# A vision tower with a mixture of experts: gate turns and bias products become stages of TensorE's order

## What is computed

```python
x2 = layernorm(x, ln2_g, ln2_b).reshape(B * S, H)
probs = softmax(x2 @ wr)                      # 64 experts
gate_v, gate_i = top_k(probs, 2)              # two experts for each token
pos = ...                                     # the token's place in its expert's buffer
buf = zeros((E, C, H)).at[ef, posc].add(tok)  # C = 72 rows for each expert
h = gelu(einsum('ech,ehf->ecf', buf, w1) + b1[:, None, :])
y = einsum('ecf,efh->ech', h, w2) + b2[:, None, :]
moe_out = (y[ef, posc] * (gf * keep)[:, None]).reshape(T, TOP_K, H).sum(axis=1)
```

## Time and profile before

| | |
|---|---|
| median of 3 runs | 390.56 us (388.23 to 392.81) |
| profiled execution | 389.98 us, of which the span of the core 388.3 |
| granted TensorE clock, mean | 0.959 |
| busy: PE, DVE, ACT, POOL | 347.7, 233.7, 220.9, 197.4 us |
| DMA | 50.20 MB, mean 129 GB/s |

### The profile page before, as it was taken

How to read it: one execution, slowest core, us unless ns; L and a number is a source line. 1 busy time by engine, 2 the same in 40 slices (tenths; PEclk the granted TensorE clock), 3 DMA queues, 4 the chain that set the end, 5 groups by cost and what they waited for, 6 DMA issues and landing times.

```text
span 388.3 us, 11371 instructions
## 1 busy us (share of the span) xinstructions
PE 347.7 (90%) x4424; PEld 315.2 (81%) x4424; DVE 233.7 (60%) x615; ACT 220.9 (57%) x640; POOL 197.4 (51%) x312
## 2 busy tenths in 40 slices
PE   8969799999988999997899899499999999999950
PEld 8748687887866889696778788399999999999950
DVE  1446788763489899897868985623335433333314
ACT  1247677777659876677488563103555555555520
POOL 3169687587841112236345767720555555555550
PEclk9999999999999999998999999559999999999995
DMA  7999924000000000000000100037899989999206
GB/s 277 374 391 334 150 28 125 2 2 1 2 3 0 3 3 2 3 2 3 3 3 2 33 9 13 15 95 202 272 320 316 322 308 316 327 324 314 85 9 182
DMA packets 21239, 50.20 MB, mean 129 GB/s; under 512 B 4116, under 2 KB 10340, under 8 KB 21058
## 3 DMA queue, kind: packets, MB, share of 16 engines
q1 hardware_dynamic: 18146, 46.96, 37.9%
q0 software_dynamic: 3040, 2.52, 2.4%
HBM read 43.97 MB, written 7.72 MB: 133 GB/s over the span
## 4 chain that ended last, share of the span: by engine, by line
PE 57%; DVE 12%; ACT 11%; POOL 9%; DMA 6%; issue 4%; SPq 1%; POOLq 0%; DVEq 0%
PE bank L728 34%; PE scores L728 18%; DMA lambdas<-in_lambdas 4%; ACT work L1037 4%; PE bank L803 3%; ACT norm L1037 3%; POOL rstd L613 3%; DVE mx L1266 2%; DVE stats L1203 2%; DVE work L1275 1%; ACT src L1037 1%; PE bank L979 1%; POOL rstd L611 1%; ACT xrow L1037 1%; POOL norm L664 1%
## 5 line engine op out<-in xcount | busy, mean ns | idle before, releaser
L1037 ACT ACTIVATE work<-scores,b1T 128x72 f32<-128x72 f32 x256 | 61.3, 322 | 66.9 <-PE scores L728 66.9
L728 PE MATMUL bank<-ring,work 128*72 128x128 f32 x512 | 97.3, 274 | 0.0
L720 POOL DMA_INDIRECT expert_rows<-work,put_u x64 | 59.9, 935 | 61.7 <-issue 37.7
L728 PE MATMUL scores<-work,ring 128*128 128x72 f32 x512 | 89.0, 258 | 0.2 <-ACT work L1037 0.2
L728 PEld LDWEIGHTS scores<-work,ring 128*128 128x128 f32 x512 | 76.9, 191 | 0.3 <-issue 0.3
L728 PE MATMUL bank<-wT 128*128 128x128 f32 x504 | 72.3, 283 | 2.7 <-ACT work L1037 2.7
L728 PEld LDWEIGHTS bank<-wT 128*128 128x128 f32 x504 | 63.8, 193 | 5.7 <-ACT work L1037 3.1
L1037 ACT ACTIVATE work<-bank 128x288 f32<-128x288 f32 (+3 forms) x136 | 46.7, 376 | 34.4 <-PE bank L728 27.0
L1437 DVE TENSOR_SCALAR work<-bank,work 72x128 f32<-72x128 f32 x64 | 22.2, 347 | 67.5 <-PE bank L728 67.5
L728 PEld LDWEIGHTS bank<-ring,work 128*72 128x72 f32 x512 | 53.8, 145 | 0.2 <-ACT work L1037 0.2
L611 POOL TENSOR_SCALAR rstd<-mv 96x3 f32<-96x3 f32 x32 | 10.1, 315 | 54.8 <-DVE mv L1206 53.6
(11 more groups left out here) (159 smaller groups left out, 594.2 us busy)
## 6 DMA issues: line engine op xcount, KB each, us to landing
ring<-in_experts SPq DMA_DIRECT2D x64, 512.0 KB, 5.0
work<-in_patches SPq DMA_DIRECT2D x3, 864.0 KB, 10.6
slot_rows<-hid SPq DMA_DIRECT2D x1, 2340.0 KB, 30.2
work<-slot_rows SPq DMA_DIRECT2D x7, 292.5 KB
wT<-in_weights SPq DMA_DIRECT2D x1, 1664.0 KB, 13.9
expert_rows<-mid POOLq DMA_DIRECT2D x2, 576.0 KB, 5.1
ring<-expert_rows SPq DMA_DIRECT2D x4, 288.0 KB, 4.0
expert_rows<-work,put_u POOLq DMA_INDIRECT x64, 4.4
```

Of the source, the lines that this page charges most:

```text
L720: pool.indirect_dma_start(out=ytok[:, :], out_offset=bass.IndirectOffsetOnAxis(ap=put_u[:, e:e + 1], axis=0), in_=ys[0:CAP, e % NY, :], in ...
L728: return nc.tensor.matmul(o, a, b, start=start, stop=stop)
L1037: return nc.scalar.activation(o, i, f, **kw)
```

## The change

The gate turns and bias products become two stages, gate_turn and gate_bias, in TensorE's order. Those of batches 0, 1 and 2 stand before rt_count:3, except the product of batch 2, right behind it; those of batch 3 follow. Turns use two banks of `scores` by turns, products 0 and 1 two others, and products 2 and 3 the banks 0 and 1 once their last jobs are taken. ScalarE instead of DVE copies the turned gates. Two tables of unread matmuls change: six instead of ten ahead of rt_turn:3 and two new ones ahead of rt_count:3; and behind each of the six row writes four instead of three, at the end ten instead of four. The waits of the expert loop on the bias sums follow the new banks.

```diff
-HEAD_WARM = 4
-PACE = 3
+HEAD_WARM = 10
+PACE = 4
...
-    moe_v:3 rt_turn:2 rt_logits:2 moe_flip:3 moe_pv:3 moe_out:3 rt_count:2 rt_turn:3 rt_logits:3 rt_count:3
+    moe_v:3 rt_turn:2 rt_logits:2 moe_flip:3 moe_pv:3 moe_out:3 rt_count:2 gate_turn:0 gate_turn:1 rt_turn:3 rt_logits:3 gate_turn:2 gate_bias:0 gate_bias:1 rt_count:3 gate_bias:2 gate_turn:3 gate_bias:3
...
-    moe_out:3=2 rt_count:2=9 rt_turn:3=10 rt_logits:3=3
+    moe_out:3=2 rt_count:2=9 rt_turn:3=6 rt_logits:3=3 rt_count:3=2
...
+            def spare(i):
+
+                name, count = taken(jobs[[n for n in range(len(jobs)) if n % 4 == i][-1]])
+                pe.wait_ge(S[name], count)
+                return banks[i]
...
+                elif stage == "gate_turn":
+
+                    pe.wait_ge(S["exp_in"], len(soft_n))
+                    pe.wait_ge(S["gm_ready"], b + 1)
+                    if b >= 2:
+                        pe.wait_ge(S["gmT_ready"], b - 1)
+                    for i in range(TPB):
+                        last = nc.tensor.transpose(scores[0:E, b % 2, TP * i:TP * i + TP], gm[:, TPB * b + i, :], const("ident")[0:TP, 0:TP])
+                    last.then_inc(S["gm_turned"], 1)
+                elif stage == "gate_bias":
+
+                    pe.wait_ge(S["gmT_ready"], b + 1)
+                    o = scores[:, 2 + b, :] if b < 2 else spare(b - 2)
+                    for i in range(TPB):
+                        last = mm(o[0:TP, D * i:D * i + D], gmT[:, b, TP * i:TP * i + TP], b2nat[:, :])
+                    last.then_inc(S["bias_full"], 1)
...
-            bias_turn(0)
-            bias_turn(1)
-            bias(0, banks[0])
-            bias_turn(2)
-            bias(1, banks[1])
-            bias_turn(3)
-            bias(2, scores[:, 2, :])
-            bias(3, scores[:, 3, :])
+            pe.wait_ge(S["gmT_ready"], NB)
...
-                        pe.wait_ge(S["bias_added"], 3)
+                        pe.wait_ge(S["bias_added"], 1)
...
-                    pe.wait_ge(S["bias_added"], min(f + 1, 2))
+                    pe.wait_ge(S["bias_added"], min(f + 3, 4))
...
+                elif stage == "gate_turn":
+                    act.wait_ge(S["gm_turned"], b + 1)
+                    go(gmT[:, b, :], scores[0:E, b % 2, 0:TB]).then_inc(S["gmT_ready"], 1)
...
-            for b in range(NB):
-                bias_in(b)
             dve.wait_ge(last_sent[2 * TPB - 1], 16)
-            bias_add(0, banks[0])
-            bias_add(1, banks[1])
-            bias_add(2, scores[:, 2, :])
-            bias_add(3, scores[:, 3, :])
+            bias_add(0, scores[:, 2, :])
+            bias_add(1, scores[:, 3, :])
+            bias_add(2, banks[0])
+            bias_add(3, banks[1])
```

More of the change, by code:

```diff
@@ L206 @@
     moe_v:2 rt_gate:0 moe_norm_b:3 rt_norm_b:1 moe_turn:3 rt_turn:1 rt_logits:1 moe_qk:3 rt_gate:1 moe_flip:2
-    moe_pv:2 moe_scores:3 rt_norm_b:2 moe_v:3 rt_turn:2 rt_logits:2 moe_flip:3 rt_gate:2 moe_pv:3 rt_norm_b:3
-    rt_turn:3 rt_logits:3 rt_gate:3
+    moe_pv:2 moe_scores:3 rt_norm_b:2 moe_v:3 rt_turn:2 rt_logits:2 moe_flip:3 rt_gate:2 moe_pv:3 gate_turn:0 gate_turn:1 rt_norm_b:3
+    rt_turn:3 rt_logits:3 gate_turn:2 rt_gate:3 gate_turn:3
     """,
@@ L956, in _ @@
                     last.then_inc(filled(job), 1)
-            def bias_turn(b):
-                pe.wait_ge(S["gm_ready"], b + 1)
-                if b >= 1:
-                    pe.wait_ge(S["gmT_ready"], b)
-                for i in range(TPB):
-                    last = nc.tensor.transpose(scores[0:E, 3, TP * i:TP * i + TP], gm[:, TPB * b + i, :], const("ident")[0:TP, 0:TP])
-                last.then_inc(S["gm_turned"], 1)
-            def bias(b, o):
-                pe.wait_ge(S["gmT_ready"], b + 1)
-                for i in range(TPB):
-                    last = mm(o[0:TP, D * i:D * i + D], gmT[:, b, TP * i:TP * i + TP], b2nat[:, :])
-                last.then_inc(S["bias_full"], 1)
             def x_turn(e):
@@ L1388, in _ @@
                     v.tensor_tensor(gm[:, t, :], oh[:, t, 0, :], oh[:, t, 1, :], ALU.add).then_inc(S["gm_ready"], 1)
-            def bias_in(b):
-                dve.wait_ge(S["gm_turned"], b + 1)
-                v.tensor_copy(gmT[:, b, :], scores[0:E, 3, 0:TB]).then_inc(S["gmT_ready"], 1)
             def bias_add(b, o):
```

## The result

The changed kernel takes 386.48 us (median of 20 runs, 383.62 to 391.43), the kernel before 390.65 us in the same session (20 runs, 388.23 to 393.46). The ratio is 0.991, with a 95% interval of 0.989 to 0.993: a gain of 3.7 us, between 2.9 and 4.5. The ratio leaves out executions in a slower state, which three of the changed kernel's showed; the quotient of the two medians, which leaves out none, is 0.989. That is within 1% or at its edge; within 1% was forecast. It is a little more than the 2.8 us of the sum. The profiled execution of after took 384.09 us against 389.98.

The account below looks back on a forecast made before the run. The start of the expert stage, set by TensorE's unread matmuls behind the last row write, was taken as the bound. Starting them at 251.0 gains 2.9 us, less 0.1 for a later count: 387.5 us predicted, range 385.6 to 390.2.

Parts of the forecast that it names:

- the sum: Start of the experts: unread matmuls from 251.0 end at 261.1 instead of 263.95; gain 2.9 less 0.1, so 2.8 us.
- items 3, 4 and 5: The first of these: turn 2 and products 0 and 1 fit TensorE's 2.88 us idle before the last count, hidden by 0.4.
- item 5: Behind the last count: product 2, last gates, turn 3, copy and product 3 leave TensorE free between 250.4 and 251.4.
- item 4: First write waits on GpSimd's copy and DVE's slots alike; faster count brings nothing, late one costs fully; +0.1 us for items 2-4.
- The clock's return (step of the sum): Clock rises 4.21 us into the unread matmuls, at 255.2, with 10.1 done; the other 23.9 take 5.9 us.
- The rival "no backlog": Clock stays up or is back before 254; first expert turn at 260.3, gain 3.6 us; chance 0.12.
- The rival "late clock": Clock returns only at 258 under the unread matmuls, which end at 262.5; gain 1.4 us, 389.1; chance 0.18.
- the rival "count pushed back": Low clock from 242.3 puts the last count at 246.7, writes 1.5 us late; gain 1.3 us, 389.2; chance 0.08.
- The rows' transfer: SyncE's read of the second chunk, needed by the third turn, done by about 259.5, 1.6 us ahead of 261.1; no wait.
- The rival with 0.08: Read's notice comes 2.1 us after its packets, so the third turn starts at 261.6; gain 2.3 us, 388.2; chance 0.08.
- item 2: ScalarE copies turned gates 0 and 1 just ahead of rt_norm_b:3, delaying row preparation 0.05 us, bounds 0 and 0.4.
- The experts' stage: Expert stage and write-back keep their length, 124.6 us from 263.68 to the end.

Follow-up runs that it names:

- d_dve: Changed kernel with the four copies of turned gates on DVE again instead of ScalarE; 386.55 us, 0.994 of the kernel before.
- first set: Four follow-up kernels run on one chip, where the kernel before takes 399.42 us; ratios 0.994 to 1.008.
- a_again: Changed kernel unedited, run again on the chip of the first set; 399.11 us, 1.000 of the kernel before.
- s_stages: Changed kernel with 3 unread matmuls behind each write and 4 at the end, instead of 4 and 10; 399.05 us, 1.001 of the kernel before.
- c_late: Changed kernel with bias products 0 and 1 put back behind the last count; 385.59 us, 0.991 of the kernel before.
- s2: s_stages again, on the chip of the second set; 387.37 us, 0.991 of the kernel before.
- n_none: Changed kernel with no unread matmuls behind the writes or at the end; 389.19 us, 0.998 of the kernel before.
- h4b: h_head4 again, on a third chip; 385.19 us, 0.990 of the kernel before.
- a2: Changed kernel unedited, run again on the chip of the second set; 387.95 us, 0.994 of the kernel before.
- h_head4: Changed kernel with 4 instead of 10 unread matmuls at the end; 396.99 us, 0.994 of the kernel before, on the first set's chip.
- second set: Kernel before, changed kernel and two variants in unread matmuls on another chip, where the kernel before takes 389.95 us; variants and changed kernel 0.991 to 0.998.
- k35: Changed kernel with 4 instead of 10 unread matmuls at the end and first read chunks of 3 and 5 experts, not 2 and 6; 385.61 us, 0.991.

## Why the prediction came out right, and where its steps were off

Each time of the forecast is counted from the last batch's turn, at 240.50 in the profile of before.

| step | forecast | after |
|---|---|---|
| last count starts | +4.7 | +4.72 |
| last write starts | +14.1 to +14.3 | +14.32 |
| unread matmuls start | +10.5 (10.0 to 10.9) | +10.51 |
| clock back at 1.00 | +14.7 | +14.36 |
| first expert turn (the sum's 261.1 is the unread matmuls' end) | +20.6 | +19.96 (their end +20.10) |
| third expert turn (0.8 behind the first, as before) | +21.4, no wait | +20.78, 0.48 us of wait |

**Nothing gained by the stages at the writes, all of it behind them (items 3, 4 and 5).** Right. The last write did not come earlier in any kernel but by 0.1 us (d_dve), and in the three of the first set it came 2.5 us later, with the stall. The unread matmuls start where the waits of item 5 put them. Bias products at full clock cost 1.55 us for twelve records; 1.5 was taken.

**A faster count brings nothing (item 4).** Right, and it is seen: the slots are done at 6.68 us behind the turn in after (244.21 + 0.16), at 7.03 before (247.37 + 0.16), 0.35 us sooner, since the clock stayed up through the count; the write still waits for GpSimd's own copy. But item 4 missed that the faster count moves DVE's next operation ahead of that copy. The copy of six elements a row starts 0.09 us behind DVE's L1389 in after and takes 0.51 us; before, it took 0.20, and in d_dve, where L1389 starts only at 247.99 and the copy at 247.83, 0.20. The same holds in all seven new-order profiles with an early L1389 (0.49 to 0.51). So the first write comes 0.28 us late and the last 0.18, where item 4 had 0.1 in all: near in size, but by another way than the one named. The Trainium skill, SBUF — State Buffer, section SBUF: two separate sides, says that a DVE operation with two SBUF inputs and a GpSimd one that reads SBUF share a port pair, and that whichever starts first keeps it for its whole length. The trace agrees: the copy ends at 245.08, just behind L1389's end at 244.48 + 0.56 = 245.04.

**The clock's return (step of the sum).** Right in kind, 0.35 us off: 3.85 us of unread matmuls at half clock instead of 4.21. The 24 others took 5.7 us, up to their end, instead of the 5.9 worked out from 0.248 each. Together they end 0.5 us sooner than forecast; the first turn's start, 0.14 us ahead of that end in the trace, is 0.6 sooner than the table's +20.6. That this step came so near is partly luck: the sum took one measured rise for a constant, and over the thirteen profiles that have unread matmuls the clock rose between 2.6 us (a_again) and 5.5 us (s_stages) into them. By the prices of 0.417 and 0.248 us a matmul I estimate that spread at 1.2 us of the first turn, about as much as separates the forecast from its rivals. The rival "no backlog" was wrong: the clock was at 0.50 when the unread matmuls began. Yet its first turn, +19.8, lies nearer to the measured +19.96 than the forecast's, so the time by itself would not have told the two apart. Its evidence did hold for the count, though not because of the unbroken stretch, as c_late shows. The rival "late clock" and the rival "count pushed back" did not come.

**The rows' transfer: the term that was most mis-sized.** The prediction had the rows there at 259.5, 1.6 us ahead of the first turn and so 2.4 ahead of the third, and no wait. In after they came last at the third turn, level with DVE's scaling to 0.05 us, so the error cost the sum nothing that shows; with fewer unread matmuls (s2, n_none, h4b) it is the read that sets the third turn.

The read's first issue is at 254.18 and the third turn at 258.47, 4.3 us later; the forecast had counted packets only, and allowed 2.7 us (256.8 to 259.5). In s2 and n_none, where TensorE is not the limit, the same distance is 3.4 and 3.5 us: 0.7 to 0.8 us more than the packet count allowed (whether ahead of the first packet or behind the last wasn't taken apart).

The rival with 0.08 had named the right cause, a notice later than the packets, but its price doesn't hold: it set a third turn at 261.6 against the point 263.95 before, which belongs to the first turn. Against the third turn before, 264.56, it is a gain of 3.0 us and no loss to the forecast.

The other 0.8 to 0.9 us of after go with something else. In the stretch 254.2 to 260.0 its queues are

```profile
q1 hardware_dynamic: 308, 0.83, 52.2%
q8 instruction: 1, 0.02, 1.4%
```

(packets, MB, share of the 16 engines), and in s2 from 253.4 to 260.0 there is no q8. The same view of SyncE as above, for s2:

```profile
L570 SPq DMA_DIRECT2D work<-slot_rows x9: 332/369/555, 253.4 to 256.8; - x9
```

An instruction load falls into the read in all five profiles with four unread matmuls behind a write and ten at the end in the new order (after, a2, a_again, c_late, d_dve). In each, one issue takes 1.1 to 2.0 us. In the other nine there is no such load and no issue over 0.56 us. The distance from the last write to the third turn (6.5 to 6.9 us in the five) is no measure of it, since 34 unread matmuls lengthen it too: h_head4, without a load and with DVE ending the wait, has 6.48.

The transfer of the piece that the third turn needs is such a measure: the chain that ended last gives it, from the start of its issue to its landing, 3.87 us in after, 4.08 in a2, 4.04 in d_dve and 4.31 in c_late, against 2.93 in s2, 3.12 in n_none, 3.25 in s_stages and 3.38 in h4b. So the load goes with a landing 0.5 to 1.4 us later. In c_late that delays the third turn; in after, a2, a_again and d_dve DVE's scaling ends within 0.1 us of the rows or later. That load, long issue and late landing go together is shown; that the load is the cause wasn't tested by itself, nor why it falls there with this number of unread matmuls.

**ScalarE's copies and row preparation (item 2).** Forecast 0.05 us late. The last batch's first row operation waits 0.20 us for GpSimd in after, so the copies ahead of it cost nothing:

```profile
236.28 1.26 ACT L1036 ACTIVATE xrow<-src,rstd 96x128 f32<-96x128 f32 x3 [0.20 <-POOL rstd L615]
```

**The experts' stage** is unchanged, as forecast (123.9 us behind the third turn, 123.7 before).

The sum had 2.8 us, the profile shows 3.3 ahead of the third turn and 3.1 to the end. The measured 3.7 (2.9 to 4.5) and, in the second set, 0.6% (0.1 to 1.0%, about 2.3 us) both hold the profile's 3.1; the sum's 2.8 lies in the second and just below the first. On the first set's chip the gain was nothing, which no mechanism of the prediction covered.

## What to carry to other kernels

Where two chains end within a tenth of a microsecond of each other, count both before you move work off one: here, by the forecast's working, the moved work was worth 3.3 us only since unread matmuls stood behind both (no run has the old order without them), and the moved stages alone brought it, without one more of these. Matmuls that only keep the clock up have a price and no sure number: without any, the next stage ran at half clock for 7.7 us and lost 3 us or more; 22 kept the clock there in one profile (s_stages) and lost it for 3.4 us in another (s2); 28 kept it in h4b and k35; 34 kept it in after, a2, a_again and d_dve and lost it in c_late. One profile of each kernel doesn't tell what the right number is, and the times don't either. When a wait names a transfer, look at what else the waiting instruction needs before you blame the transfer. Time a read from its first issue to its user in a kernel where nothing else is late, not by its packets.

## What the runs showed of the hardware

- The clock did not rise in n_none from 258.6 to 266.3 under experts that kept TensorE busy (7.39 of 7.40 us in the stretch shown), nor under turns and bias products before. Under unread 128x128 matmuls it rose after 3.85 us in after and 4.21 before, and anywhere from 2.6 us (a_again) to 5.5 us (s_stages) in the others. What sets these apart the runs don't say.
- The clock fell under experts that kept TensorE busy, behind a wait for rows ahead of the third turn: 2.6 us behind that turn in c_late (wait of 1.23 us), 1.5 in s2 (1.07). It did not fall behind such waits of 1.55 us in h4b and 1.10 in s_stages.
- GpSimd's copy of 96x6 elements took 0.20 us alone and 0.5 us with a DVE operation of 0.56 us begun 0.1 us ahead.
- One SyncE issue among nine took 1.1 to 2.0 us instead of 0.37 in the five profiles in which an instruction load of 0.02 MB fell among them, and the piece that the third turn needs landed 0.5 to 1.4 us later than in four without.
- On one of the chips, waits of 1 to 4 us stood on DVE and ScalarE that end on nothing the trace names, and the kernel before took 9.5 to 10.5 us more than on the chips of the other two sets.
